# A two-layer graph attention kernel: in layer 0 both projection blocks of a step ahead of the next scores

## The reference

```python
m = embs @ map_w.T + map_b
sem = m.reshape(b, s, h, dk).transpose(0, 2, 1, 3)
n = sem / jnp.maximum(jnp.linalg.norm(sem, axis=-1, keepdims=True), COS_EPS)
cos = jnp.einsum('bhsd,bhtd->bhst', n, n) * (~sm)
cos_adj = (cos > THRESHOLD)
q = (m @ q_w.T + q_b) ; k = (m @ k_w.T + k_b)      # split into heads
scores = jnp.where(sm, NEG, q @ k.T / sqrt(dk))
adj = cos_adj * jax.nn.softmax(scores, axis=-1) * keep
Ax = jnp.einsum('hbst,hbtd->hbsd', adj_h, sem_h)   # sem_h = embs @ gcn_map_w.T + gcn_map_b
out = relu((Ax @ gcn_W.T) / (adj_h.sum(-1, keepdims=True) + 1.0))
```

## Time and profile before

| what | value |
|---|---|
| median of the runs (3) | 2652.82 us |
| the profiled execution | 2656.29 us |
| its span, first to last instruction | 2654.5 us |
| TensorE busy | 2587.7 us, 97% |
| VectorE, ScalarE, GpSimd busy | 1990.9, 1754.5, 1399.6 us |
| mean granted clock of TensorE | 0.994 |
| first matmuls of the groups' steps in layer 0 | from 108.95 to 1715.67 us, 30 groups |

### The profile page before, as it was taken

The page is one execution under the profiler, slowest core; times in us unless marked ns, Lnnn a source line. Parts: engine busy times, 40 slices in busy tenths (PEclk is TensorE's granted clock), DMA queues, the critical chain, the costliest instruction groups (busy, mean ns, idle before and its releaser), DMA issues. The chain is left out here.

```text
span 2654.5 us, 62516 instructions
## 1 busy us (share of the span) xinstructions
PE 2587.7 (97%) x20882; PEld 1393.6 (52%) x20886; DVE 1990.9 (75%) x6361; ACT 1754.5 (66%) x5020; POOL 1399.6 (53%) x2790
## 2 busy tenths in 40 slices
PE   6999999999999999999999999997999999999998
PEld 3455555555555555555555555554555555555554
DVE  6477778777877777777777777786777777777766
ACT  3566666666666666666666666675777777777774
POOL 4255545545554555555555555544565656555552
PEclk9999999999999999999999999998999999999999
DMA  5367766776667666766776677678786777778774
GB/s 141 61 136 158 144 135 133 149 155 130 145 141 140 145 128 144 149 142 133 141 147 141 131 140 146 148 141 195 158 175 160 169 163 170 164 160 170 158 149 102
DMA packets 945489, 387.43 MB, mean 146 GB/s; under 512 B 857617, under 2 KB 859153, under 8 KB 945169
## 3 DMA queue, kind: packets, MB, share of 16 engines
q1 hardware_dynamic: 945168, 383.44, 69.0%
HBM read 114.86 MB, written 67.11 MB: 69 GB/s over the span
## 5 line engine op out<-in xcount | busy, mean ns | idle before, releaser
L552 ACT ACTIVATE probs<-probs,negmax 128x128 f32<-128x128 f32 x1024 | 398.2, 390 | 455.6 <-DVE negmax L124 455.6
L465 POOL TENSOR_TENSOR o_sb<-o_sb,xres 128x512 f32<-128x512 f32 x127 | 161.5, 1272 | 496.5 <-DVE o_sb L739 493.1
L166 PE MATMUL l_ps_pj<-hT,room 128*128 128x512 f16 x1488 | 346.7, 383 | 2.3 <-ACT room L1343 2.3
L166 PE MATMUL ps_pj<-wm_hi,hT 128*128 128x512 f16 x1024 | 326.4, 380 | 12.6 <-DVE wm_lo L761 6.8
L166 PE MATMUL ps_pj<-wv_hi,hT 128*128 128x512 f16 x1024 | 326.4, 380 | 0.0
L166 PE MATMUL ps_pj<-hT,wk_hi 128*128 128x512 f16 x1024 | 305.9, 380 | 0.0
L166 PE MATMUL ps_pj<-hT,wq_hi 128*128 128x512 f16 x1024 | 304.5, 379 | 0.0
L1357 ACT ACTIVATE l_probs<-l_probs,l_negmax 128x128 f32<-128x128 f32 x512 | 199.2, 390 | 139.0 <-DVE l_negmax L124 138.8
L1292 POOL TENSOR_TENSOR l_h<-l_h 128x512 f16<-128x512 f32 x120 | 139.6, 1164 | 282.3 <-DVE l_out_sb L1440 245.0
L124 DVE CUSTOM_DVE_ANT_0 probs<-ps_sc,mask 128x128 f32<-128x128 f32 x1024 | 235.4, 285 | 47.4 <-PE ps_sc L981 46.7
L721 DVE SCALAR_TENSOR_TENSOR c<-cprobs,c 128x512 f16<-128x512 f32 x256 | 185.2, 723 | 79.6 <-ACT c L559 79.2
(11 more groups left out here) (172 smaller groups left out, 6198.8 us busy)
## 6 DMA issues: line engine op xcount, KB each, us to landing
xg<-in_x SPq DMA_DIRECT2D x128, 256.0 KB, 3.4
xres<-in_x SPq DMA_DIRECT2D x128, 256.0 KB, 3.1
x_scratch<-o_sb SPq DMA_DIRECT2D x128, 256.0 KB, 2.4
out<-l_out_sb SPq DMA_DIRECT2D x128, 256.0 KB, 3.3
l_ring<-x_scratch SPq DMA_DIRECT2D x124, 256.0 KB, 3.2
mask_u<-in_adj SPq DMA_DIRECT2D x64, 64.0 KB, 2.8
cpT<-c SPq DMA_TRANSPOSE x256, 3.2
xg<-x_scratch SPq DMA_DIRECT2D x12, 256.0 KB, 3.2
```

The costliest lines, as they stand in the source:

```text
L166: last = pe.matmul(out, a(kt), b(kt), start=(n == 0), stop=(n == 3 * kts - 1))
L465: nc.gpsimd.tensor_tensor(o_sb[:, j % 2], o_sb[:, j % 2], xres[:, j % 2], ALU.add).then_inc(res_done, 1)
L552: last = nc.scalar.activation(probs[:, i], probs[:, i], ACT.Exp, bias=negmax[:, u % 2, i:i + 1], scale=-1.0, accum_out=zsum[:, u % 4, hh:h ...
```

## The change

Three orders change, and no instruction is added or removed. On TensorE the second projection block goes ahead of the scores. On VectorE `row_max(n + 1)` goes behind the copies of both projection blocks. On ScalarE `k_copy` goes ahead of `exps(n + 1)`. The last group of layer 0 keeps its own order.

```diff
@@ ScalarE, group(t) @@
                     if proj and u >= KT:
                         q_copy(t + 1, u - KT)
+                    if proj and u >= KT:
+                        k_copy(t + 1, u - KT)
                     if n + 1 < 8 * GROUPS:
                         exps(n + 1)
-                    if proj and u >= KT:
-                        k_copy(t + 1, u - KT)
@@ VectorE, group(t) @@
                     p_low(n)
-                    row_max(n + 1)
                     if u < QUAD:
                         m_copy(t + 1, u)
...
                     if u < QUAD:
                         v_copy(t + 1, u)
+                    row_max(n + 1)
                     weight1_step(t, u)
@@ TensorE, group(t) @@
                         project_q(t + 1, u - QUAD)
-                    scores(n + 1)
                     weight1_norms(t, u)
                     if u < QUAD:
                         project_v(t + 1, u)
                     else:
                         project_k(t + 1, u - QUAD)
+                    scores(n + 1)
                     if n >= 2:
                         norms_read(t, u)
                         weigh_values(n - 2)
```

## The result

The changed kernel takes 2831.97 us (median of 4 runs, 2829.82 to 2834.82) where the kernel before took 2654.06 in the runs beside it: a ratio of 1.067, 95% interval 1.065 to 1.069. The profiled execution took 2829.98 us. From the first `m` matmul of one group to that of the 30th after it, the kernel before took 1606.7 us and the changed one 1775.6, 168.9 more; what follows (the 31st such group, the last group and layer 1) took 944.8 instead of 938.8.

A forecast was written before the change was run, and what follows sets the result against it. TensorE was taken to bound layer 0, at 6.63 us a step. Stops of 5.4 us a group over 31 groups gave 167 us on 2656.3, so 2823, less 3.5 to the median: 2820 us, range 2700 to 2852.

The forecast's parts named there:

- TensorE's pace and the seam: TensorE in layer 0: a step stays 6.63 us where nothing waits; the new matmul-height switch costs zero, +-22 us.
- The closed chain: VectorE, ScalarE, steps 1 and 2: row maxima to row maxima become one loop, 6.74 us, 7.24 with the port.
- The port: VectorE's `p_low` waits for GpSimd's `v_low` on the shared SBUF ports, 0.50 us more a step; `normalise` blocks too.
- The stops: TensorE ahead of a group's four `q` blocks: waits of 2.3, 1.3, 0.3 and 1.5 us, 5.4 a group.
- the groups that prepare a weight: Four groups where TensorE waits for a reduction behind the row maxima: about 1 us more each, within the rounding.
- Layer 1 keeps its time: Layer 1 starts with no buffer of the changed order in its way, so no time is added there.
- The clock: Sign against the forecast: TensorE's granted clock in layer 0 leaving 1.00.
- The rival of 2980: TensorE's stops also make the clock fall, 5 us lost in each group: 2980 us instead of 2820; chance 0.08.
- no difference: Rival: `v_low` stays clear, links are 2% shorter, step 3's stretch is taken up, TensorE keeps pace: 2653 us; chance 0.05.
- faster: Rival: the seam from scores to weighted values hides the change of height, 0.09 us a step: 2631 us; chance 0.05.

The follow-up runs named there:

- e6_low_v_and_norm_wait: The changed kernel with GpSimd's `v_low` waiting for `p_low` of its step and each `normalise` pair for `p_low` of the next step: 2708.41 us.
- e8_m_copy_ahead_too: The changed kernel with `relu` and `h_high` ahead of the next step's exponentials, `h_low` behind the row maxima, `m_copy` right behind `select_similar`: 2657.24 us.
- e12_m_copy_alone: The changed kernel with `m_copy` right behind `select_similar` and nothing else: 2762.73 us.
- e1_tensor_only: The kernel before with only TensorE's order changed, the scores behind the second projection block: 2932.93 us.

## Why the prediction was right

The median came 12 us above 2820, inside the range. The forecast was 167 us more in 31 groups; the profiled executions differ by 173.7, of which 168.9 lie in the first 30 groups, 4.6 in the 31st and 4.1 in the last group, while layer 1 took 2.8 less and what runs ahead of the groups 1.1 less. Groups of 58.5 us were forecast, and their median is 59.1. Step by step:

- **TensorE's pace and the seam.** The step is still 6.63 where nothing waits (1067.71 to 1074.34), and the seam is the zero that was taken.
- **The closed chain.** Forecast 7.24, measured 7.16. By start to start: maxima to exponentials 0.95, exponentials 1.57, `square` and `v_high` 1.03, `p_high` 0.66, `p_low` 1.10 with its wait for the port, `m_copy` 0.66, head sums 0.60, `v_copy` 0.59. Most of the 0.08 is the head sums, which I had at 0.65.
- **The port.** Forecast 0.50, measured 0.50. That `normalise` holds `p_low` up as the other tiles do, the part that rested least on rows, is shown by the 0.55 of 1207.00 and the 27 us of `e6_low_v_and_norm_wait`. By the Trainium skill, "SBUF — State Buffer", section "SBUF: two separate sides", the later one of such a pair blocks until the first is over; the traces agree for `v_low`, `normalise` and `add_residual`, which have two inputs as well, and in both directions: the `v_low` of 1206.41 began while `p_low` ran and took 1.56 instead of 1.12. It does not agree for a GpSimd tile with one input, which reads SBUF too and held nothing up (the last section); there the measurement decides.
- **The stops.** Forecast 2.3, 1.3, 0.3 and 1.5, 5.4 a group; measured in the short group 2.12, 1.19, 0.16 and 1.38, 4.85. Each term is 0.1 to 0.2 too large, in the direction of the 0.08 that each round of the chain was over-sized by. Over the 30 groups the `q` blocks' stops sum to 123 us, 4.1 a group, since in the groups with a stretch at half clock (below) that stretch takes the place of some of them.
- **What filled the difference, and was not forecast.** Stops ahead of `m` blocks, 24.9 us against 8.6 before; the groups that prepare a weight, 8.2 against 5.4, which I had called rounding; and 51.2 us at half clock, which lengthen the matmuls in them by 25.6. Then 123 + 16.3 + 2.8 + 25.6 = 168 of the 168.9. The sum of 5.4 a group was met by a smaller first term and three others, and to that extent its closeness is luck. Most of the `m` stops follow late loads of `xg`, but not all: 8.2 of the 24.9 us lie in groups ahead of which VectorE did not wait for a load, nearly all of it in the first 15 groups, among which are the four that prepare a weight. `e8_m_copy_ahead_too` and `e12_m_copy_alone` show that the place of `m_copy` makes the stops; what makes `xg` late, which in `e1_tensor_only` it hardly is (1.8 us), stays open.
- **Layer 1 keeps its time.** From its first matmul of scores to the end it takes 841.7 us, where it took 844.5. The last group of layer 0, which the sum left out, takes 43.2 instead of 39.0 from its first projection block on, and TensorE stops there once more:

```profile
1949.99 2.32 PE L166 MATMUL ps_pj<-hT,room 128*128 128x512 f16 x5 [2.09 <-ACT room L590]
```

- **The clock.** I had put down a granted clock other than 1.00 in layer 0 as a sign against the forecast, and it did leave it. In 14 groups the stop ahead of the first `q` block was followed by a stretch at 1.2 GHz, half speed, and in the groups there is one such stretch elsewhere. One of them in the windows, and its group in TensorE's timeline:

```profile
1267.20:1270.60 3.40, 3.40 (x10) 1.22 (x8) 2.40 (x13) 2.18 (x10) 1.27 (x1) 0.50 0.99 143
```

```profile
1266.41 0.60 PE L166 MATMUL ps_pj<-hT,wq_hi 128*128 128x512 f16 x2 [2.04 <-DVE m_sb L682]
...
1270.70 0.60 PE L166 MATMUL ps_pj<-hT,wk_hi 128*128 128x512 f16 x2
...
1274.74 0.59 PE L166 MATMUL ps_pj<-hT,wq_hi 128*128 128x512 f16 x2
```

The `q` block takes 4.29 us instead of 2.6. But the next `q` block, which in the short group stopped for 1.19 us, follows without a stop: the chain sets its time, not TensorE, and so the 1.7 us fill waits that were there. Groups with such a stretch last no longer than the others: of two without any `m` stop one has a stretch and lasts 58.00 us, the other has none and lasts 57.99; and two with `m` stops of 0.61 and 0.45, one with a stretch and one without, last 59.12 each. The rival of 2980 priced the lost speed as if TensorE still set the pace. The rivals of no difference and of faster fall with the chain: both needed it under 6.63.

## What to carry to other kernels

An engine at 97% hides the others only as long as every hand-over that crosses it has its slack; before moving work on it, write the hand-overs as one loop, start to start, and compare the sum with the step. Once the loop is the longer one, half a microsecond at any link of it (here a collision of VectorE and GpSimd) is paid in full, and the cure is to take links out of it rather than to speed up the busy engine. TensorE's order was itself neutral once the loop was the shorter one (2644.6 against 2645.0 us). What beat the kernel before, by 10 us, were edits to VectorE and ScalarE alone: a copy taken earlier, and a weight step and an instruction that waits for a load moved out from ahead of the links; how much of it is due to which was not measured.

## What the runs showed of the hardware

TensorE came to the first `q` block of a group out of an otherwise full stream each time. Of the 27 stops there of 2.1 to 2.2 us, 14 were followed by a half-clock stretch; none of the four of 1.6 us was, nor any of the 31 of 1.5 to 1.8 us there in `e1_tensor_only`; and the 2.83 us stop of the earlier trace rows left the clock at 1.00. But one stop of 1.84 us ahead of an `m` block of `e1_tensor_only` was followed by such a stretch (granted clock 0.50 from 1185.9 us on). So the length of one stop does not tell whether the clock falls.

The exclusion between GpSimd and VectorE holds for VectorE instructions with two SBUF tiles, not for the others in the same places: 32 times in the changed kernel `head_sums` (one SBUF tile) began inside a `v_low`, and each time it took its usual 0.67 us. Nor does it hold against every GpSimd tile. In the changed kernel's GpSimd and VectorE timelines, the mask conversion (L439), which has one input, and an `h_low` begun inside it:

```profile
1228.13 1.50 POOL L439 TENSOR_SCALAR mask<-mask_u 128x512 bf16<-128x512 uint8 x1
```

```profile
1229.17 0.69 DVE L677 TENSOR_TENSOR h<-h 128x512 f16<-128x512 f32 x1 [1.13 <-ACT h L518]
```

The mask conversion ends at 1229.63, and `h_low` takes its undisturbed 0.69. All 31 such pairs of this kernel are alike: `h_low` ends 0.23 or 0.24 us after the conversion, not 0.55.
